# A gated delta rule in eleven pipelined stages: gates as 32 more value columns, two-part logs, 19-column weights, and another order at each stage's start

## The chip, the cores and the metric

The kernel runs on one core of one Trainium2 chip. The metric is device microseconds from start to end of one execution. Engines: PE (TensorE, matmuls; PEld is its weight load), DVE (VectorE), ACT (ScalarE), POOL (GpSimd) and SP, which issues DMAs. Each has its own queue and runs it in order; they meet by semaphores. PE's granted clock stands at one of two levels, 1.2 and 2.4 GHz, shown as 0.5 and 1.0.

## The reference

A two-layer tower over 64 images with 38 tokens of 256 features. Only the attention of the second layer changes. It is a recurrence over the 38 tokens of an image, per head (16 heads of 16 features):

```
q, k, v = silu(x @ Wq), l2norm(silu(x @ Wk)), silu(x @ Wv)
gk      = log_sigmoid(x @ Wf)               # one number per token and head
a       = k * -sigmoid(x @ Wgamma) * exp(gk)
for t in tokens:
    Sp = S * exp(gk[t])
    u  = a[t] @ Sp + v[t]
    S  = Sp + outer(k[t], u)
    o[t] = q[t] @ S
```

After it come a gate (sigmoid of a rank-16 product), a layer norm, the product with Wo and the second feed-forward.

## The kernel before

**The method.** No loop runs over tokens. With decays D[t, s] = exp(sum of gk between s and t), u solves (I - A) u = v, where A[t, s] = D (a_t . k_s), and o = (D (q . k)) u. The inverse of I - A is built row by row for the two halves of 19 tokens; the halves are joined by a remainder.

**The stages.** Images are worked off in 8 chunks of 8 (`CB`); a chunk is four pairs of images (`IP`), so 64 lanes of image pair and head. `last_layer` first normalises and transposes x (`layer_norm_turn`, which also loads and splits the weights into a high and a low fp32r part), then calls `delta_stage` eleven times (`CHUNKS + 3`). One stage works on four chunks at once, each a step further on:

- `nxt` (stages 0 to 7): `project` makes q, k and the two gates with features on partitions, in 8 projections of 6 matmuls of 304 columns; `sigmoid`, `silu_of`, then the norm of the keys (`square` on POOL, `key_norm` on PE, `bounded`, `inverse_norms`, `unit_key`), `gates` and `a_of` for a.
- `c` (stages 1 to 8): `values` makes v and the forget logit (24 matmuls of 272 columns); `forget_parts`, `forget_logs`, `log_forget` give gk; `steps` on POOL, `decay` on PE and ACT give D; `score` on PE and `weigh` on DVE give q.k and a.k times D in `PA`.
- `z` (stages 2 to 9): `a_rows` on PE turns A so that lanes stand on partitions (banks 0 and 1), a copy by ACT and one by DVE bring it into `AS`; `inverse_row(1..18)` on DVE, each a product and a reduction, each waiting for the one before; `inverse_out` and `inverse_back` turn the inverse back into `TS`.
- `y` (stages 3 to 10): `first_half`, `first_back`, `remainder`, `with_values`, `second_half`, `solution` solve for u (banks 0 and 1); `output` gives o, and `high_out` and `low_out` write it as two parts.

Stages 3 to 7 hold all four and are called full; a middle stage is one of 4 to 7. A stage ends with a barrier of all engines, and the first product of the next needs the last `weigh`.

**The order.** It is written out by hand: the last lines of the four engine programs call those functions one after another (before: lines 1625 to 1664 for PE, 1781 to 1819 ACT, 1950 to 1990 DVE, 2041 to 2063 POOL). Scores use banks 0 to 3 alone, so `score(p + 1)` waits for `weigh(2p)` and `weigh(2p + 1)`, and they for it. `steps(b + 2)` waits for `decay(b)` of PE, `decay(b + 2)` for it.

## Time and profile before

| | |
|---|---|
| runs | median 2027.8 us (2023.66, 2027.8, 2028.45) |
| the profiled execution | 2023.3 us, span 2021.3 |
| busy, whole span | PE 1769.4, DVE 1084.5, ACT 672.3, POOL 299.6 us |
| normalisation ahead of the stages | 1280.9 to 1304 us |
| stages 0 to 10 | 1304 to 1850 us |
| PE's first matmul in stages 3 to 8 | 1399.8, 1466.8, 1529.7, 1593.0, 1656.7, 1720.5 |
| mean granted clock | 0.876 of 2.4 GHz |

Times in a timeline count from the span's start. A wait is named by what ended it; "issue" is time in which the engine waited for nothing that the profile shows. A group's busy time adds durations, which overlap a little on one engine, so the distance from start to start is the better price of an instruction in a row of them.

### The profile page before, as it was taken

The numbers are of one execution on the slowest core, as the hardware profiler recorded it, in microseconds if no ns is written. First come the engines' busy times: TensorE is split into PE (matmuls) and PEld (weight loads), VectorE is DVE, ScalarE is ACT, GpSimd is POOL, SyncE is SP. The second block draws the span as 40 slices with busy tenths as digits, with TensorE's granted clock in tenths as the row PEclk, the third lists the DMA queues.
The fourth block names the chain that finished last, engine by engine and source line by source line (L and its number), as shares of the span: only waits on it lengthen the run. The fifth ranks groups of instructions, "written<-read, shape, count | busy, mean of one in ns | idle before, by whom it ended". The sixth has DMA issues, their size and how long they took to land. (4 is left out here: it accounts for less than half of the span.)

```text
span 2021.3 us, 52149 instructions
## 1 busy us (share of the span) xinstructions
PE 1769.4 (88%) x22817; PEld 1573.1 (78%) x22817; DVE 1084.5 (54%) x2346; ACT 672.3 (33%) x1389; POOL 299.6 (15%) x302
## 2 busy tenths in 40 slices
PE   5677786799999999999999999778999889777589
PEld 4466675579888999999999989566788778767468
DVE  3655555584546545545555455545534454442885
ACT  3344444432223222223223232354333333223133
POOL 0322232610000000000000000332222222100540
PEclk9788898899999999999999999788776877655579
DMA  4100000100001000000000000100000000001001
GB/s 142 50 2 1 0 0 2 65 21 22 22 1 43 1 22 21 22 22 22 22 21 22 1 1 1 34 2 2 3 4 3 3 3 4 4 4 47 1 7 44
DMA packets 9943, 36.03 MB, mean 18 GB/s; under 512 B 3056, under 2 KB 5896, under 8 KB 7176
## 3 DMA queue, kind: packets, MB, share of 16 engines
q1 hardware_dynamic: 9736, 32.96, 4.7%
q8 instruction: 167, 2.74, 0.6%
q14 instruction: 40, 0.33, 0.1%
HBM read 30.47 MB, written 2.49 MB: 16 GB/s over the span
## 5 line engine op out<-in xcount | busy, mean ns | idle before, releaser
L1042 ACT ACTIVATE hidden<-bank,moe_b 128x512 f32<-128x512 f32 (+1 forms) x320 | 213.3, 668 | 537.1 <-PE bank L934 526.1
L951 PE MATMUL bank<-moe_w2h,hidden_hi 128*128 128x256 f32 x1216 | 345.7, 284 | 0.0
L951 PE MATMUL bank<-moe_w2l,hidden_hi 128*128 128x256 f32 x1216 | 344.0, 283 | 0.0
L951 PE MATMUL bank<-moe_w2h,hidden_lo 128*128 128x256 f32 x1216 | 344.0, 283 | 0.0
L934 PE MATMUL bank<-x_hi,moe_w1h 128*128 128x512 f32 (+1 forms) x640 | 243.8, 381 | 2.9 <-ACT hidden L1042 2.8
L934 PE MATMUL bank<-x_lo,moe_w1h 128*128 128x512 f32 (+1 forms) x640 | 242.5, 379 | 0.0
L934 PE MATMUL bank<-x_hi,moe_w1l 128*128 128x512 f32 (+1 forms) x640 | 242.0, 378 | 0.0
L951 PEld LDWEIGHTS bank<-moe_w2h,hidden_hi 128*128 128x128 f32 x1216 | 233.1, 192 | 5.9 <-DVE residual L1076 4.3
L951 PEld LDWEIGHTS bank<-moe_w2l,hidden_hi 128*128 128x128 f32 x1216 | 233.2, 192 | 1.2
L951 PEld LDWEIGHTS bank<-moe_w2h,hidden_lo 128*128 128x128 f32 x1216 | 233.2, 192 | 0.0
L1076 DVE SCALAR_TENSOR_TENSOR residual<-bank,gates,residual 128x256 f32<-128x256 f32 x152 | 73.4, 484 | 290.4 <-PE bank L951 290.4
L1064 DVE TENSOR_TENSOR hidden_lo<-hidden,hidden_hi 128x512 fp32r<-128x512 f32 (+1 forms) x320 | 215.2, 672 | 11.0
L1062 DVE CAST hidden_hi<-hidden 128x512 fp32r<-128x512 f32 (+1 forms) x320 | 133.1, 416 | 87.3 <-ACT hidden L1042 79.9
L934 PEld LDWEIGHTS bank<-x_hi,moe_w1h 128*128 128x128 f32 x640 | 120.3, 188 | 25.8 <-ACT hidden L1042 5.0
L934 PEld LDWEIGHTS bank<-x_hi,moe_w1l 128*128 128x128 f32 x640 | 120.1, 188 | 20.4
L934 PEld LDWEIGHTS bank<-x_lo,moe_w1h 128*128 128x128 f32 x640 | 120.3, 188 | 18.7
L1249 POOL MEMSET gate_low<- 80x2432 f32 x1 | 2.1, 2121 | 867.1 <-POOLq L68 867.1
L167 PE MATMUL bank<-ident,normed_tiles 128*128 128x128 f32 x152 | 49.7, 446 | 47.6 <-DVE normed_tiles L136 47.6
L167 PEld LDWEIGHTS bank<-ident,normed_tiles 128*128 128x128 f32 x152 | 22.5, 204 | 74.1 <-DVE normed_tiles L136 74.0
L2008 POOL TENSOR_TENSOR decay_steps<-normed_tiles,from_here 128x304 f32<-128x304 f32 x64 | 50.5, 804 | 139.6 <-PE bank L1506 73.9
L1902 DVE TENSOR_TENSOR qk_and_ak<-bank,decay 128x304 f32<-128x304 f32 x128 | 52.2, 466 | 22.5 <-ACT decay L1722 17.0
L831 POOL TENSOR_TENSOR probs<-probs,row_inv 128x608 f32<-128x608 f32 x32 | 38.7, 1209 | 167.1 <-DVE row_inv L715 166.9
(284 smaller groups left out, 3531.5 us busy)
## 6 DMA issues: line engine op xcount, KB each, us to landing
moe_w<-in_moe_w SPq DMA_DIRECT2D x16, 1024.0 KB, 4.8
patches<-in_patches SPq DMA_DIRECT2D x8, 864.0 KB, 4.5
out<-residual SPq DMA_DIRECT2D x19, 128.0 KB, 1.7
ffn_w<-in_ffn_w SPq DMA_DIRECT2D x2, 1024.0 KB, 6.4
att_w<-in_att_w SPq DMA_DIRECT2D x1, 1536.0 KB, 5.9
delta_w<-in_delta_w SPq DMA_DIRECT2D x1, 1280.0 KB
tok_w<-in_tok_w SPq DMA_DIRECT2D x1, 768.0 KB, 4.1
delta_wvf<-in_delta_wvf SPq DMA_DIRECT2D x1, 272.0 KB
```

Source lines behind the costliest of these rows:

```text
L167: turn = nc.tensor.transpose(bank[t % 4][:, m * P:(m + 1) * P], XN[:, t % 4, m * P:(m + 1) * P], ident[:, :])
L831: nc.gpsimd.tensor_tensor(PR[:, p % 2, :, 0:SEQ], PR[:, p % 2, :, 0:SEQ], spread(RI[:, p % 2, :], 2, SEQ), ALU.mult).then_inc(normed, 1)
L934: mm = nc.tensor.matmul(bank[i % 4][:, 0:n], left, right, start=(j == 0), stop=(j == len(passes) - 1))
L951: mm = nc.tensor.matmul(bank[4 + n % 3][:, 0:D], left, right, start=(i == 0), stop=(i == len(passes) - 1))
L1042: nc.scalar.activation(H[:, i % 4, 0:n], bank[i % 4][:, 0:n], ACT.Relu, bias=b1[:, x, f:f + 1]).then_inc(acted, 1)
L1062: nc.vector.tensor_copy(HH[:, k % 2, f, 0:n], H[:, i % 4, 0:n]).then_inc(h_hi, 1)
L1064: nc.vector.tensor_tensor(HL[:, k % 2, f, 0:n], H[:, i % 4, 0:n], HH[:, k % 2, f, 0:n].bitcast(F32), ALU.subtract).then_inc(h_lo, 1)
L1076: nc.vector.scalar_tensor_tensor(out=RES[:, t, :], in0=bank[4 + n % 3][:, 0:D], scalar=G[:, t, x:x + 1], in1=RES[:, t, :], op0=ALU.mult, o ...
L1249: nc.gpsimd.memset(G1[:].bitcast(F32), 0.0).then_inc(done, 1)
L1902: nc.vector.tensor_tensor(PA[:, c % 2, p, m * HPH:(m + 1) * HPH].rearrange("p (g e) x t -> p e g x t", e=2)[:, e], psum[:, 0:PPH, n * 2 * ...
L2008: nc.gpsimd.tensor_tensor(MS[:, b % 2], spread(LZ[:, 3, b // 2, b % 2 * HPH:(b % 2 + 1) * HPH], 2, SEQ), spread(here[:, :], 1, HPH), ALU.m ...
```

## The change

- **Gates.** The two gate projections per half (4 of 8 projections) go, and so do `gates` and `a_of`. The weight of `values` gets 16 more columns (Wgamma, one per head), so v, forget logit and gamma logit come as token rows: 288 columns. `step_scale` makes g = -sigmoid(gamma) sigmoid(f) for 64 lanes. PA then holds k.k in place of a.k, and g is applied where rows are turned: `a_rows` turns g too (4 matmuls more), and `a_out` on DVE copies it and multiplies the 18 rows by it in one product of 684 elements, in place of the two copies; `with_values` becomes two products on DVE.
- **Split logs.** gk is split into two fp32r parts, `steps` writes both (608 elements for 304), and `decay` adds two fp32r matmuls in place of one fp32 matmul. Four decay buffers stand for two; v has three for two.
- **19-column weights.** `first_half` and `second_half` load 19 columns of `TS` for 32.
- **The order.** See below. In the normalisation, two weight splits fewer follow, which move two tiles later with the wait for the loads.

```diff
-        wh = sb(ctx, "delta_wh", [P, 5, HALVES, D], F32R)
+        wh = sb(ctx, "delta_wh", [P, 3, HALVES, D], F32R)
-DECAYS = 2
+DECAYS = 4
+KINDS = D + 2 * HEADS
...
-        "MS": sb(ctx, "decay_steps", [P, 2, HPH, SEQ]),
+        "MS": sb(ctx, "decay_steps", [P, 2, 2, HPH, SEQ], F32R),
...
-    jobs = ((K, 0), (K, 1), (Q, 0), (Q, 1), (GAMMA, 0), (F, 0), (GAMMA, 1), (F, 1))
+    jobs = ((K, 0), (K, 1), (Q, 0), (Q, 1))
...
-                nc.tensor.matmul(bank[4 + b % 2][:, 0:CT], after[:, :],
-                                 MS[:, b % 2].rearrange("p g t -> p (g t)"),
-                                 start=False, stop=True).then_inc(d_log, 1)
+                for part in range(2):
+                    mm = nc.tensor.matmul(bank[4 + b % 2][:, 0:CT], after[:, :],
+                                          MS[:, b % 2, part].rearrange("p g t -> p (g t)"),
+                                          start=False, stop=(part == 1))
+                mm.then_inc(d_log, 1)
...
+                for r in range(4):
+                    nc.tensor.matmul(psum[half(r // 2), r % 2, 0:HALF],
+                                     GZ[block_rows(r), z % 3].rearrange("p i g -> p (i g)"),
+                                     ident[block_rows(r), r * HB:r * HB + HALF], start=True, stop=True)
...
             def first_half(j):
...
                 if z is not None:
-                    pe.wait_ge(a_taken, 2)
+                    pe.wait_ge(a_taken, 1)
...
-                        mm = nc.tensor.matmul(psum[rows, j, place(lane)],
-                                              TS[rows, lane * HALF:lane * HALF + HB], vh_y[rows, lane, :],
+                        mm = nc.tensor.matmul(psum[PAD * s:PAD * s + HALF, j, place(lane)],
+                                              TS[rows, lane * HALF:(lane + 1) * HALF], vh_y[rows, lane, :],
...
-            def a_of_second():
+            def a_out():
...
-                nc.vector.tensor_copy(AS[:, 1, 1:HALF].rearrange("p t s -> p (t s)"),
-                                      bank[1][:, HALF:HALF * HALF]).then_inc(a_taken, 1)
+                nc.vector.tensor_copy(AS[:, :, 0, :], psum[:, 0:2, 0:HALF]).then_inc(scale_in, 1)
+                dve.wait_ge(scale_in, 1)
+                nc.vector.tensor_tensor(AS[:, :, 1:HALF, :],
+                                        psum[:, 0:2, HALF:HALF * HALF].rearrange("p h (t s) -> p h t s", s=HALF),
+                                        spread(AS[:, :, 0, 1:HALF], 3, HALF), ALU.mult).then_inc(a_taken, 1)
...
+            def step_scale():
...
+                nc.vector.scalar_tensor_tensor(
+                    out=GZ[:, c % 3], in0=SV[:, :, D + HEADS:KINDS], scalar=-1.0, in1=SV[:, :, D:D + HEADS],
+                    op0=ALU.mult, op1=ALU.mult).then_inc(scale_ready, 1)
...
-                nc.vector.tensor_tensor(RX[:, lanes(j), :], vh_y[:, lanes(j), :],
-                                        bank[j][:, :].rearrange("p (l d) -> p l d", d=HD),
+                scale = GZ[:, y % 3].rearrange("p i g -> p (i g)")
+                nc.vector.tensor_tensor(RX[:, lanes(j), :], bank[j][:, :].rearrange("p (l d) -> p l d", d=HD),
+                                        spread(scale[:, lanes(j)], 2, HD), ALU.mult).then_inc(r_scaled, 1)
+                dve.wait_ge(r_scaled, j + 1)
+                nc.vector.tensor_tensor(RX[:, lanes(j), :], RX[:, lanes(j), :], vh_y[:, lanes(j), :],
                                         ALU.add).then_inc(rx_ready, 1)
...
-                nc.gpsimd.tensor_tensor(MS[:, b % 2], spread(LZ[:, 3, b // 2, b % 2 * HPH:(b % 2 + 1) * HPH], 2, SEQ),
-                                        spread(here[:, :], 1, HPH), ALU.mult).then_inc(steps_ready, 1)
+                heads = slice(b % 2 * HPH, (b % 2 + 1) * HPH)
+                nc.gpsimd.tensor_tensor(MS[:, b % 2], spread(LF[:, :, b // 2, heads].bitcast(F32), 3, SEQ),
+                                        spread(spread(here[:, :], 1, HPH), 1, 2), ALU.mult).then_inc(steps_ready, 1)
```

**PE, how a full stage comes to its first solution product.** Before, the stage opens with `a_rows` (L1549), and the values' 24 matmuls (L1492) stand between it and the first half (L1581); a projection (L1474) follows.

```order
L1492 MATMUL bank<-delta_wvfl,dchunk_hi 128x272
L1492 MATMUL bank<-delta_wvfh,dchunk_lo 128x272
L1581 MATMUL bank<-values,inverse_t 32x16 x128
L1474 MATMUL bank<-x_hi,delta_wh 128x304
L1474 MATMUL bank<-x_lo,delta_wh 128x304
```

The same place now. Values and projections 0 and 1 (L1476) open the stage.

```order
L1476 MATMUL bank<-x_lo,delta_wh 128x304
L1476 MATMUL bank<-x_hi,delta_wl 128x304
L1551 MATMUL bank<-ident,step_scale 64x19 x4
L1557 MATMUL bank<-ident,qk_and_ak 64x19 x72
L1589 MATMUL bank<-values,inverse_t 19x16 x128
L1601 MATMUL bank<-u_then_rest,qk_and_ak 19x16 x64
```

The turn of the coefficients has moved right before the first half, which has 19 columns, and the remainder (L1601) follows at once.

**PE, around the output product.** Before, the output (L1621) and four projections are followed by key norms (L1483), two decays (L1504, L1506), a score (L1528) and a turn of the inverse (L1564).

```order
L1474 MATMUL bank<-x_hi,delta_wl 128x304
L1483 MATMUL bank<-k_square_then_norm,same_head 128x304 x2
L1504 MATMUL bank<-past,ident_bf_8 128x304
L1506 MATMUL bank<-decay_steps,after 128x304
L1504 MATMUL bank<-past,ident_bf_8 128x304
L1506 MATMUL bank<-decay_steps,after 128x304
L1528 MATMUL bank<-q_and_a_92,dk_in_pair 64x76 x32
L1564 MATMUL bank<-ident,inverse 64x64 x16
```

Now (L1613 is the second half, L1629 the output, L1485 the key norms, L1506 and L1509 a decay, L1532 a score):

```order
L1613 MATMUL bank<-u_then_rest,inverse_t 19x16 x64
L1506 MATMUL bank<-past,ident_bf_8 128x304
L1509 MATMUL bank<-decay_steps,after 128x304 x2
L1613 MATMUL bank<-u_then_rest,inverse_t 19x16 x64
L1506 MATMUL bank<-past,ident_bf_8 128x304
L1509 MATMUL bank<-decay_steps,after 128x304 x2
L1485 MATMUL bank<-k_square_then_norm,same_head 128x304 x2
L1629 MATMUL bank<-qk_and_ak 32x38 x128
L1506 MATMUL bank<-past,ident_bf_8 128x304
L1509 MATMUL bank<-decay_steps,after 128x304 x2
L1532 MATMUL bank<-q_and_k_91,dk_in_pair 64x76 x32
```

Two decays and the key norms stand ahead of the output, and no projection stands behind it.

**DVE, behind the output's low parts.** Before (L1922 the low parts, L1837 and L1840 a row of the inverse, L1874 the bounded norms, L1902 a weighing product):

```order
L1922 TENSOR_TENSOR x_lo<-bank,x_hi 128x4x38 x4
L1837 TENSOR_TENSOR normed_tiles<-a_rows,inverse 128x2x14x14
L1840 TENSOR_REDUCE inverse<-normed_tiles 128x2x14
L1874 TENSOR_SCALAR k_square_then_norm<-bank 128x304 x2
L1837 TENSOR_TENSOR normed_tiles<-a_rows,inverse 128x2x15x15
L1840 TENSOR_REDUCE inverse<-normed_tiles 128x2x15
L1902 TENSOR_TENSOR qk_and_ak<-bank,decay 128x4x76 x2
L1837 TENSOR_TENSOR normed_tiles<-a_rows,inverse 128x2x16x16
```

Now (L1918 the low parts, L1832 and L1835 a row, L1895 a weighing product, L1882 the unit keys):

```order
L1918 TENSOR_TENSOR x_lo<-bank,x_hi 128x4x38 x4
L1832 TENSOR_TENSOR normed_tiles<-a_rows,inverse 128x2x13x13
L1835 TENSOR_REDUCE inverse<-normed_tiles 128x2x13
L1832 TENSOR_TENSOR normed_tiles<-a_rows,inverse 128x2x14x14
L1835 TENSOR_REDUCE inverse<-normed_tiles 128x2x14
L1895 TENSOR_TENSOR qk_and_ak<-bank,decay 128x4x76 x4
L1832 TENSOR_TENSOR normed_tiles<-a_rows,inverse 128x2x15x15
L1835 TENSOR_REDUCE inverse<-normed_tiles 128x2x15
L1882 TENSOR_TENSOR q_and_k_91<-q_and_k_91,k_square_then_norm 128x8x38 x2
L1832 TENSOR_TENSOR normed_tiles<-a_rows,inverse 128x2x16x16
```

The bounded norms have left this place, row 13 has come in, and behind row 16 stand two weighing pairs and rows 17 and 18, then the last four pairs in a row; before, the a-products stood between them.

## Rows read from the trace of the kernel before

**Rows 1.** Windows, one stage each: us, then PE, PEld, DVE, ACT, POOL busy, PEclk
```profile
1354.00:1398.00 44.00, 35.15 (x576) 29.49 (x576) 27.31 (x69) 18.76 (x45) 11.57 (x16) 0.84 0.01 2
1398.00:1465.00 67.00, 60.12 (x1600) 53.64 (x1600) 28.97 (x75) 22.35 (x55) 14.26 (x18) 0.69 0.01 3
...
1591.50:1655.00 63.50, 56.53 (x1600) 50.26 (x1600) 28.75 (x75) 22.23 (x55) 14.27 (x18) 0.76 0.01 3
```

**Rows 2.** Windows of PE alone, the middle stage: us, PE busy, PEclk
```profile
1610.00:1632.00 22.00, 22.00 (x681) 0.50 0.02 4
...
1636.00:1655.00 19.00, 16.61 (x369) 1.00 0.01 3
```

**Rows 3.** Timeline of PE, middle stage: start, us, line, x count [idle before <-releaser]
```profile
1593.04 5.06 PE L1549 MATMUL bank<-ident,qk_and_ak 32*64 32x19 f32 x144 [2.62 <-PEq L68]
...
1602.98 3.17 PE L1581 MATMUL bank<-values,inverse_t 32*32 32x16 f32 x189
...
1616.47 0.62 PE L1474 MATMUL bank<-x_hi,delta_wh 128*128 128x304 f32 x1
...
1618.29 3.60 PE L1605 MATMUL bank<-u_then_rest,inverse_t 32*32 32x16 f32 x128
...
1634.27 1.10 PE L1621 MATMUL bank<-qk_and_ak 64*32 64x38 f32 x103 [1.85 <-issue]
```

**Rows 4.** Timeline of PE, the stage without projections
```profile
1737.51 2.31 PE L1593 MATMUL bank<-u_then_rest,qk_and_ak 32*19 32x16 f32 x128 [1.62 <-issue]
1740.98 1.48 PE L1593 MATMUL bank<-u_then_rest,qk_and_ak 32*19 32x16 f32 x79 [1.16 <-issue]
...
1744.45 3.60 PE L1605 MATMUL bank<-u_then_rest,inverse_t 32*32 32x16 f32 x128 [0.82 <-issue]
```

**Rows 5.** Timeline of DVE, the middle stage
```profile
1598.16 0.52 DVE L1827 COPY a_rows<-bank 128x342 f32<-128x342 f32 x1 [6.03 <-PE bank L1549]
...
1627.25 0.51 DVE L1837 TENSOR_TENSOR normed_tiles<-a_rows,inverse 128x338 f32<-128x338 f32 x1
...
1643.71 1.21 DVE L1837 TENSOR_TENSOR normed_tiles<-a_rows,inverse 128x578 f32<-128x578 f32 x1
...
1654.14 1.62 DVE L1902 TENSOR_TENSOR qk_and_ak<-bank,decay 128x304 f32<-128x304 f32 x4 [1.10 <-ACT decay L1722]
```

**Rows 6.** Groups of DVE, tail of the middle stage: busy us, mean ns | idle before, releaser
```profile
L1902 DVE TENSOR_TENSOR qk_and_ak<-bank,decay 128x304 f32<-128x304 f32 x16 | 6.5, 466 | 2.7 <-ACT decay L1722 2.7
L1837 DVE TENSOR_TENSOR normed_tiles<-a_rows,inverse 128x392 f32<-128x392 f32 (+4 forms) x5 | 3.9, 779 | 0.0
L1840 DVE TENSOR_REDUCE inverse<-normed_tiles 128x28 f32<-128x392 f32 (+4 forms) x5 | 3.5, 692 | 0.2
...
L1874 DVE TENSOR_SCALAR k_square_then_norm<-bank 128x304 f32<-128x304 f32 x2 | 0.9, 470 | 0.3 <-PE bank L1483 0.3
...
L1888 DVE SCALAR_TENSOR_TENSOR q_and_a<-dk_t,sig_gamma 128x304 f32<-128x304 f32 x2 | 0.8, 466 | 0.0
```

**Rows 7.** Timeline of POOL there, and from the page a 608-element product
```profile
1643.61 0.70 POOL L2008 TENSOR_TENSOR decay_steps<-normed_tiles,from_here 128x304 f32<-128x304 f32 x1 [2.75 <-PE bank L1506]
...
L831 POOL TENSOR_TENSOR probs<-probs,row_inv 128x608 f32<-128x608 f32 x32 | 38.7, 1209 | 167.1 <-DVE row_inv L715 166.9
```

**Rows 8.** Timeline of PE, first stage with values and no inverse
```profile
1325.86 0.57 PE L1492 MATMUL bank<-delta_wvfh,dchunk_hi 128*128 128x272 f32 x1 [4.03 <-PEq L68]
...
1334.74 0.41 PE L1474 MATMUL bank<-x_hi,delta_wh 128*128 128x304 f32 x1 [2.61 <-DVE dk_t L1856]
```

**Rows 9.** Timeline of DVE, the very first stage
```profile
1321.03 0.47 DVE L1874 TENSOR_SCALAR k_square_then_norm<-bank 128x304 f32<-128x304 f32 x1 [1.21 <-PE bank L1483]
```

**Rows 10.** Timeline of DVE, the normalisation ahead of the stages
```profile
1289.51 0.61 DVE L1237 TENSOR_SCALAR delta_w<-delta_w,norm_w 128x256 f32<-128x256 f32 x2 [1.86 <-DMA from_here<-in_from_here]
...
1293.52 0.40 DVE L136 TENSOR_SCALAR normed_tiles<-residual,mean_var,std 128x256 f32<-128x256 f32 x1
...
1296.81 1.03 DVE L136 TENSOR_SCALAR normed_tiles<-residual,mean_var,std 128x256 f32<-128x256 f32 x1
```

More of the change, by code:

```diff
@@ L1221, in last_layer @@
         same = sb(ctx, "same_head", [P, P])
-        after = sb(ctx, "after", [P, P])
+        after = sb(ctx, "after", [P, P], F32R)
         past = sb(ctx, "past", [P, SEQ], BF16)
@@ L1258, in last_layer @@
                             splits=[(wg[:], wgh[:], wgl[:]), (wvf[:], wvfh[:], wvfl[:])]
-                            + [(w[:, n], wh[:, n], wl[:, n]) for n in range(5)])
+                            + [(w[:, n], wh[:, i], wl[:, i]) for i, n in enumerate((0, 1, 4))])
         with ExitStack() as inner:
@@ L1380, in delta_buffers @@
         "PA": sb(ctx, "qk_and_ak", [P, 2, IP, HEADS, 2, SEQ]),
-        "VH": sb(ctx, "values", [P, 2, IP, HEADS, HD]),
-        "QA": [sb(ctx, f"q_and_a{i}", [P, HALVES, CB, 2, SEQ]) for i in range(2)],
-        "KT": sb(ctx, "dk_t", [P, HALVES, CB, SEQ]),
+        "VH": sb(ctx, "values", [P, 3, IP, HEADS, HD]),
+        "QK": [sb(ctx, f"q_and_k{i}", [P, HALVES, CB, 2, SEQ]) for i in range(2)],
         "SH": sb(ctx, "dchunk_hi", [P, HALVES, CB, PAD], F32R),
@@ L1628, in _ @@
             low_part(0)
+            low_part(1)
+            project(0)
+            project(1)
+            a_rows()
             first_half(0)
             first_half(1)
-            project(0)
-            low_part(1)
+            low_part(2)
             remainder(0)
-            project(1)
-            low_part(2)
-            remainder(1)
             project(2)
             low_part(3)
-            second_half(0)
+            remainder(1)
             project(3)
             low_part(4)
+            second_half(0)
+            decay(0)
             second_half(1)
-            project(4)
-            project(5)
-            output()
-            project(6)
-            project(7)
+            decay(1)
             key_norm(0)
             key_norm(1)
-            decay(0)
-            decay(1)
+            output()
+            decay(2)
             score(0)
+            decay(3)
             inverse_out(0)
-            decay(2)
+            decay(4)
+            score(1)
+            decay(5)
             inverse_out(1)
-            decay(3)
-            score(1)
+            decay(6)
+            score(2)
+            decay(7)
             inverse_out(2)
-            decay(4)
-            decay(5)
-            score(2)
-            decay(6)
-            decay(7)
             score(3)
@@ L1950, in _ @@
             decay_masks()
-            a_of_second()
+            log_forget()
+            silu_of(0)
+            silu_of(1)
+            a_out()
             for t in range(1, 6):
                 inverse_row(t)
-            log_forget()
-            inverse_row(6)
-            with_values(0)
-            silu_of(0)
-            inverse_row(7)
-            with_values(1)
-            silu_of(1)
             values_of(0)
             values_of(1)
-            inverse_row(8)
-            silu_of(2)
             values_of(2)
             values_of(3)
-            inverse_row(9)
+            with_values(0)
+            silu_of(2)
+            with_values(1)
             silu_of(3)
             gate_parts()
-            for t in range(10, 14):
+            step_scale()
+            for t in range(6, 10):
+                inverse_row(t)
+            bounded(0)
+            bounded(1)
+            for t in range(10, 13):
                 inverse_row(t)
```

186 lines of the change are left out of this document (80 added, 106 removed).

## Prediction

> **What bounds the kernel now.** The change lies in the eleven delta stages and in the normalisation just ahead of them; nothing behind them is touched. I read the windows by stage first, then one middle stage engine by engine, then the ends. The windows [rows 1] show the first full stage at 67.0 us and a later one at 63.5, PE busy for 60.1 and 56.5 of it, DVE for 29. PE is the engine to follow, but its granted clock is now at one of its levels, now at the other: 0.50 (1.2 GHz) over 22 us of small matmuls, 1.00 (2.4 GHz) over the last 19 us [rows 2]. The timeline of PE [rows 3] splits a middle stage in two. **Front**, from the first matmul (1593.04) to the end of the output product (1634.27 + 1.10 = 1635.37): 42.3 us. **Tail**, from there to DVE's last product (1654.14 + 1.62 = 1655.76 [rows 5]): 20.4 us. In the front PE is hardly idle; in the tail it is DVE that hardly rests: of 20 us it waits 3.2 [rows 6].
>
> Two more things hide in the front. A small matmul costs by the columns of its weights: 128 with 32 columns take 3.60 us, 128 with 19 take 2.31 [rows 3, 4], 10 ns less each. And PE runs dry: the output product is broken by an "issue" idle of 1.85 us [rows 3]. In the stage without projections [rows 4] the pieces between such idles hold 128 records and start at 1737.51, 1740.98 and 1744.45: twice 3.47 us apart, however fast the piece was (2.31 us and 1.16 idle; then 2.65 and 0.82). I read this as the supply of PE's instructions: **no block of 128 records starts sooner than 3.47 us after the last.** (An fp32 product counts double in these records: 72 in the code are x144 [rows 3].)
>
> **A middle stage, front.** Values come first now, then projections 0 and 1. The stage that has this order already took from 1325.86 to 1332.13 for them (1334.74 less the idle of 2.61 [rows 8]): 6.3, less 0.2 of modelled overhang, plus 0.25 for 16 more columns in 24 matmuls: 6.35. The turns of the coefficients: 5.06 us for 144 [rows 3], now 152: 5.3. Then a new wait: the first solution product writes the two banks that DVE has to empty, and where the values stood between (1598.10 to 1602.98, 4.9 us [rows 3]) nothing does now. DVE makes a copy of 38 elements and a product of 684; a copy of 342 took 0.52 [rows 5], so 0.2 + 0.9 and hand-overs: 1.3, bounds 1.0 (the product alone) and 1.8 (at 1.5 times its price). Behind it on PE is the whole rest of the front.
>
> From there to the output's end PE has four times 256 small records, projections 2 and 3 (12), two decays (6) and the key norms (4): 1046 records, 8.17 blocks, 28.4 us at 3.47. By duration alone it would be less: 768 records of 19 columns are 6 x 2.31 = 13.9, the output 2.7 (1.10 for 103 [rows 3]), projections 3.6 (1616.47 to 1618.29 [rows 3], twice), norms and decays about 4.5: 25. So **the narrower weights gain next to nothing; the blocks take it back.** Three blocks with dense matmuls exceed 3.47 (by 0.4, 0.4 and 1.2), the cut ones at both ends are quicker (1.2): 29.2, bounds 25 and 32. Front: 6.35 + 5.3 + 1.3 + 29.2 = 42.15, against 42.3. The four projections that go (7.3 us by those rows) pay for the wait and for the norms and decays that now stand ahead of the output; the rest of them ran beside refills.
>
> **Tail.** DVE's list changes so [rows 6]: the bounded norms leave (0.9 + 0.3 of wait), the a-products leave (0.8), of the 2.7 us of waits before weighing products the last of 1.10 [rows 5] stays, 1.6 go, because two decays are done early, four decay buffers stand for two, and rows 17 and 18 stand beside a score. Row 13 comes in, 2 x 0.51 [rows 5]. POOL's steps hold 608 elements for 304: 0.70 becomes 1.2 (the page's 608-element product), bounds 1.2 and 1.6 [rows 7]. They are off the path, six of them in 18 us, but DVE's product of two SBUF operands that met one (both near 1643.7) took 1.21 us, and the five products of such rows 3.9 against 3.5 for their five reductions [rows 5 to 7]: 0.4 a meeting, which at the new length is 0.7. Four of the six steps can meet one: 2.8 at most, 0.4 is in already; I add 0.8, a third of the rest. Sum: 20.4 - 1.2 - 0.8 - 1.6 + 1.05 + 0.8 = 18.65, bounds 17.8 and 20.3. PE keeps up: of its 16.6 us in the last 19 [rows 2] the norms, two projections and two decays leave. The decays' fp32 products become two fp32r ones: nothing on the path. Between the stages nothing changes. **A middle stage gains 0.15 + 1.8, so 2.0 us, times four: 8.** The first full stage, 67.0 long [rows 1] where the others are near 63.5, lands with them at 61.5: 5.5.
>
> **The other stages.** The one with the first inverse (44.0 [rows 1]) is DVE's: coefficients ready at 6.35 + 5.3 + 1.3 = 12.95, then its 27.3 us less the evacuation, the a-products and what now runs earlier (0.5 + 0.8 + 1.1), 1.4 of hand-overs, a score 1.1, 1.0 between stages: 40.3, gain 3.7. The first with values: 24 projections of 304 columns at 2.4 GHz 3.0, a-products 0.8, and 1.2 of the 2.61 wait [rows 8], as the sigmoids of the keys no longer stand behind those of the values: 5.0. The very first: DVE was free 1.21 us before the key norms [rows 9], and the a-products go: 2.0. The last three: the blocks hold, the wait comes in, one more row in the tail, two decays fewer in one: 0.8 lost. The normalisation: DVE waited 1.86 us for loads, which now it does two tiles of 0.65 later: 1.3; its products took 1.03 instead of 0.40 while POOL split weights [rows 10], two splits fewer: 1.25; one copy more, 0.15: 2.4. **Sum: 2.4 + 2.0 + 5.0 + 3.7 + 5.5 + 8 - 0.8 = 25.8.** The profiled execution took 2023.3 us, near the fastest run; the median is 2027.8. I take the gain off the median: **2002.**
>
> **Rivals.** (1) *The full stages give nothing*: the wait is 1.8 and POOL meets every product. For it: [rows 5 to 7]. Then 25.8 - 8 - 3 = 15 remain, 2013; inside my range. (2) *No block rule*: blocks are buffered well ahead, the front falls by 4.2 us to its matmuls in five stages and by 7 in two of the last: 35 more, 1967. Against it stand the idles themselves [rows 3, 4]. The Trainium skill, Runtime: NRT & Kernel Launch, Instruction fetch mechanics, says that instructions come in blocks of 256 and that crossing a boundary is "mostly hidden"; by that rule the time is this rival's. The trace disagrees with "hidden" (1.16 us of a block), though 128 matmuls with their loads do make 256. (3) *Slower*: POOL's steps and DVE's products take turns in full. Eight steps of 1.6 instead of 0.7 add 7 us to DVE in each of eight stages, 57 - 26: 2059. It decides from 3.2 us a stage on. Against it: the weighing products, over a third of DVE's tail, read PSUM, and 0.4 of a 0.70 step was felt. The Trainium skill, SBUF — State Buffer, Who interferes with whom, lets a product of two SBUF inputs wait for a whole POOL instruction; by it a meeting costs 1.2, some 2 us more a stage, 2018. (4) *No difference*: the tail at 1.2 GHz. The dense projections that stood before it are gone; PE's 11 us of tail become up to 21, past DVE's 18.6, 3 us a stage in eight stages: 2026.
>
> **Chances.** Forecast 0.68, rival 1 0.16, rival 2 0.05, rival 3 0.04, rival 4 0.07. The range 1986 to 2018 holds the first two and with them 0.84; the bounds of the front (25 and 32, in five stages) would reach farther, at the lower end to rival 2. A measurement here tells 0.3%, 6 us, from no change: faster 0.90, same 0.05, slower 0.05.
>
> **What would show it.** Middle stages of 61 to 62 us, front 42, tail 18 to 19; PE idle for 1.3 us ahead of the first 19-column product; "issue" idles in nearly every block of the front, 3.47 us from start to start; one late wait of DVE instead of three; steps of 1.2 to 1.6 on POOL. I am wrong if blocks follow faster than 3.47, or if the tail doesn't shorten.

## The result, and the profile after

The changed kernel takes 2012.81 us, the median of four runs (2009.08 to 2015.91), and the kernel before 2027.22, the median of four as well (2023.66 to 2028.45; one run more than in the table ahead of the change): a ratio of 0.9931, 95% interval 0.9907 to 0.9955. That is 14.4 us less, where 25.8 were forecast. The time lies in the range, the sign is right, and the gain is little more than half of what the working gave. 2013 was the time of the first rival, "the full stages give nothing", and the trace says the same, though only one half of that rival's reasons holds.

The profiled execution took 2014.98 us, with a span of 2013.2. Stage by stage, from PE's first matmul to that of the next stage (for the normalisation, from DVE's first operation to its last), the two traces give:

| | before | after | gained | forecast |
|---|---|---|---|---|
| normalisation | 23.1 | 21.0 | 2.1 | 2.4 |
| stage 0 | 21.2 | 19.5 | 1.7 | 2.0 |
| stage 1 | 30.0 | 25.7 | 4.3 | 5.0 |
| stage 2, first inverse | 44.0 | 44.5 | -0.5 | 3.7 |
| stage 3, first full | 67.0 | 61.4 | 5.5 | 5.5 |
| stages 4 to 7, mean | 63.4 | 63.9 | -0.5 each | 2.0 each |
| stages 8 to 10 together | 132.2 | 132.9 | -0.7 | -0.8 |

The sum is 10.5 us. Both traces show one thing more that no edit explains: in the unchanged code ahead of the normalisation the profiled execution of after is 2.4 us later. So the two profiled spans differ by 8.1 us (2021.3 and 2013.2) and the medians by 14.4: the table places the gain of one execution of each, and some 6 us of the medians' difference stand in no row of it.

Of before, timeline of DVE: the first operation of the normalisation.

```profile
1280.94 2.11 DVE L119 TENSOR_SCALAR std<-mean_var 128x19 f32<-128x19 f32 x1 [0.78 <-PEq L68]
```

Of after, timeline of DVE, the same operation, the scaled weights and a product of a tile beside a split by GpSimd, which answer to [rows 10].

```profile
1283.34 2.11 DVE L119 TENSOR_SCALAR std<-mean_var 128x19 f32<-128x19 f32 x1 [0.78 <-PEq L68]
...
1292.25 0.61 DVE L1237 TENSOR_SCALAR delta_w<-delta_w,norm_w 128x256 f32<-128x256 f32 x2 [0.90 <-DMA from_here<-in_from_here]
...
1301.00 1.02 DVE L136 TENSOR_SCALAR normed_tiles<-residual,mean_var,std 128x256 f32<-128x256 f32 x1
```

The wait for the loads is 0.90 us for 1.86, and four products took 1.0 us for six.

**The middle stage.** Windows of after by stage (us; PE, PEld, DVE, ACT, POOL busy; PEclk), the answer to [rows 1]: PE is busy for 50.4 us of 62.9, where it was busy for 56.5 of 63.5. Six microseconds of work on the fullest engine are gone, and the stage is as long as it was.

```profile
1350.10:1394.60 44.50, 31.22 (x560) 27.74 (x561) 29.95 (x70) 17.00 (x41) 13.58 (x15) 0.73 0.01 2
1394.60:1456.00 61.40, 50.04 (x1584) 44.59 (x1585) 32.11 (x78) 20.42 (x51) 16.40 (x17) 0.67 0.02 4
1584.80:1647.70 62.90, 50.35 (x1584) 45.10 (x1584) 33.12 (x78) 20.68 (x50) 16.31 (x16) 0.66 0.01 3
```

Timeline of PE in that stage, the answer to [rows 3].

```profile
1584.81 0.58 PE L1494 MATMUL bank<-delta_wvfh,dchunk_hi 128*128 128x288 f32 x1 [2.68 <-PEq L68]
...
1592.53 5.04 PE L1557 MATMUL bank<-ident,qk_and_ak 32*64 32x19 f32 x144
...
1598.79 2.74 PE L1589 MATMUL bank<-values,inverse_t 32*19 32x16 f32 x153 [1.22 <-DVE a_rows L1821]
...
1602.43 1.81 PE L1589 MATMUL bank<-values,inverse_t 32*19 32x16 f32 x98 [0.90 <-issue]
...
1605.90 1.91 PE L1601 MATMUL bank<-u_then_rest,qk_and_ak 32*19 32x16 f32 x103 [1.23 <-issue]
...
1613.63 2.32 PE L1613 MATMUL bank<-u_then_rest,inverse_t 32*19 32x16 f32 x128
...
1616.75 2.32 PE L1613 MATMUL bank<-u_then_rest,inverse_t 32*19 32x16 f32 x128
...
1621.60 1.32 PE L1629 MATMUL bank<-qk_and_ak 64*32 64x38 f32 x129
1624.04 1.30 PE L1629 MATMUL bank<-qk_and_ak 64*32 64x38 f32 x127 [1.12 <-issue]
...
1643.70 1.40 PE L1532 MATMUL bank<-q_and_k,dk_in_pair 32*64 32x76 f32 x64 [0.56 <-DVE qk_and_ak L1895]
```

The reader sees the new wait, 1.22 us, as forecast; "issue" idles between the small products, with 3.47 us from 1602.43 to 1605.90; two second halves, each of 128 records, that start only 3.12 us apart (1613.63, 1616.75), and 129 output records that are followed by the next after 2.44 us (1621.60, 1624.04), both sooner than the 3.47 of the prediction's rule; and, at the end, a score that took 1.40 us, where one at 2.4 GHz takes 0.95. Values and projections 0 and 1 took 7.58 us (1584.81 to 1592.39; 7.2 in the mean of stages 4 to 7), for 6.35 in the sum.

Windows of PE alone in after (us, PE busy, PEclk): [rows 2] had 1.00 in the tail; here the whole tail has 0.72 and its last 7 us have 0.50.

```profile
1625.34:1646.82 21.48, 14.30 (x351) 0.72 0.01 3
...
1639.82:1646.82 7.00, 3.81 (x111) 0.50 0.01 2
```

Timeline of DVE in that tail, the answer to [rows 5].

```profile
1630.09 1.61 DVE L1895 TENSOR_TENSOR qk_and_ak<-bank,decay 128x304 f32<-128x304 f32 x4 [1.04 <-PE bank L1532]
1631.62 1.01 DVE L1832 TENSOR_TENSOR normed_tiles<-a_rows,inverse 128x450 f32<-128x450 f32 x1
...
1633.20 1.86 DVE L1882 TENSOR_TENSOR q_and_k<-q_and_k,k_square_then_norm 128x304 f32<-128x304 f32 x2
1634.99 1.70 DVE L1832 TENSOR_TENSOR normed_tiles<-a_rows,inverse 128x512 f32<-128x512 f32 x1
...
1638.85 0.75 DVE L1832 TENSOR_TENSOR normed_tiles<-a_rows,inverse 128x578 f32<-128x578 f32 x1
...
1645.20 1.62 DVE L1895 TENSOR_TENSOR qk_and_ak<-bank,decay 128x304 f32<-128x304 f32 x4 [1.55 <-issue]
```

The larger product of row 17 (578 elements) took 0.75 us, that of row 16 (512) 1.70. Timeline of POOL, beside it:

```profile
1630.94 1.21 POOL L2003 TENSOR_TENSOR decay_steps<-log_f_parts,from_here 128x608 fp32r<-128x608 f32 x1 [0.99 <-PE bank L1509]
1633.46 2.68 POOL L2003 TENSOR_TENSOR decay_steps<-log_f_parts,from_here 128x608 fp32r<-128x608 f32 x2 [1.31 <-PE bank L1509]
```

Two steps stand from 1633.46 to 1636.14, over the unit keys and the product of row 16, and the step before them, to 1632.15, over the beginning of row 15 (450 elements); no other product of this tail is late. What a product lost is nearly what was left of the step when it started: 0.4 of 0.53 us for row 15, 1.0 of 1.15 for row 16. A product that takes longer because a step runs beside it is called a meeting here, as in the prediction. Two suspects, then, for the tail: GpSimd's longer steps, and PE's clock. The question of the experiments is which, and whether they are one.

### The profile page after: what moved, and what is told of

It reads as the page before. It is cut to its first block and busy times, and to the rows that moved or that the text cites. A ratio compares the mean times of both kernels' runs of the same rounds, so it can differ in the third digit from the quotient of the medians.

```text
span 2013.2 us, 51796 instructions
## 1 busy us (share of the span) xinstructions
PE 1715.6 (85%) x22689; PEld 1525.8 (76%) x22689; DVE 1110.8 (55%) x2379; ACT 657.8 (33%) x1347; POOL 314.5 (16%) x284
## 5 line engine op out<-in xcount | busy, mean ns | idle before, releaser
L934 PEld LDWEIGHTS bank<-x_hi,moe_w1h 128*128 128x128 f32 x640 | 120.3, 188 | 25.8 <-ACT hidden L1042 5.0
L2003 POOL TENSOR_TENSOR decay_steps<-log_f_parts,from_here 128x608 fp32r<-128x608 f32 x64 | 78.5, 1236 | 150.1 <-PE bank L1509 113.0
L1832 DVE TENSOR_TENSOR normed_tiles<-a_rows,inverse 128x2 f32<-128x2 f32 (+5 forms) x144 | 67.6, 469 | 3.5
```

What stands on the lines that cost most here:

```text
L934: mm = nc.tensor.matmul(bank[i % 4][:, 0:n], left, right, start=(j == 0), stop=(j == len(passes) - 1))
L1832: nc.vector.tensor_tensor(PD[:, :, 0:t, 0:t], spread(AS[:, :, t, 0:t], 2, t), TT[:, :, 0:t, 0:t], ALU.mult).then_inc(t_mult, 1)
L2003: nc.gpsimd.tensor_tensor(MS[:, b % 2], spread(LF[:, :, b // 2, heads].bitcast(F32), 3, SEQ), spread(spread(here[:, :], 1, HPH), 1, 2), AL ...
```

## The experiments

Each kernel is the changed one with the edit shown. Times are set against the kernel before, run on the same chip, since its median moved between 2027.2 and 2025.1; a difference to the changed kernel is that of the ratios, times 2025. Its uncertainty is some 5 to 6 us, most of it from the changed kernel's own interval.

**The narrow weights undone.**

```diff
-mm = nc.tensor.matmul(psum[PAD * s:PAD * s + HALF, j, place(lane)],
-                      TS[rows, lane * HALF:(lane + 1) * HALF], vh_y[rows, lane, :],
+mm = nc.tensor.matmul(psum[PAD * s:PAD * s + HB, j, place(lane)],
+                      TS[rows, lane * HALF:lane * HALF + HB], vh_y[rows, lane, :],
```

(and so in `second_half`).

> The changed kernel with one part undone: the two halves of the solution load 32 columns of the inverse again, for 19. My theory (blocks of 128 records start no sooner than 3.47 us after one another): 128 such matmuls cost 3.60 us for 2.32, but the blocks of 19 columns end 1.1 us before the next may start, so that only 3.60 - 3.47 = 0.13 us of each is seen, four blocks a stage, seven stages: about +4 us, 2013 to 2018. The idle called issue in the front (3.9, 6.7, 4.7, 3.3 and 5.2 us in the five full stages) shrinks by some 4 us a stage. Rival (a matmul's price is what the front pays): 512 x 10 ns = 5.1 us a stage, seven stages and some: +36 to +41 us, about 2050.

Measured: 2023.46 us, 0.9984 (0.9975 to 0.9993), 10.7 us more than the changed kernel. In stages 4 to 7 the path from the first solution product to the output's end grew by 1.6 us in the mean (29.0 to 30.7), and the "issue" idle of a stage fell from 5.5 to 2.2. Timeline of PE:

```profile
1602.02 6.85 PE L1589 MATMUL bank<-values,inverse_t 32*32 32x16 f32 x250 [1.22 <-DVE a_rows L1821]
...
1617.14 3.60 PE L1613 MATMUL bank<-u_then_rest,inverse_t 32*32 32x16 f32 x128
...
1621.54 3.60 PE L1613 MATMUL bank<-u_then_rest,inverse_t 32*32 32x16 f32 x128
```

Of 5.1 us that 512 matmuls save by their own duration, a stage sees 1.6: the rest was waiting for instructions anyway. My theory had 0.5, the rival 5. The theory was too even: from one second half to the next PE took 4.40 us here (1617.14 to 1621.54) and 3.12 in the changed kernel, all that the narrow ones save, where six and three dense matmuls stand ahead of them and neither has an "issue" idle before it. From the first solution product to the projection behind the first remainder it saved 0.3 us (9.2 here, 8.95 in the changed kernel): the "issue" idles took the rest. The time itself lies between the two expectations, 5 us above the first and 27 below the second.

**Each remainder product issued twice.**

```diff
+for _ in range(2):
     mm = nc.tensor.matmul(psum[PAD * s + HB:PAD * s + HB + HALF, j, place(lane)],
                           pa_y[rows, lane, 1, HALF:SEQ], RX[rows, lane, :],
                           start=True, stop=True)
```

> The changed kernel with each of the 128 products of a remainder issued twice (the same result written twice): 256 small records of 19 columns more in each of eight stages. Block theory (no block of 128 records starts sooner than 3.47 us after the last): 2 x 3.47 = 6.9 us a stage, +55 us, about 2068, although DVE, ACT and GpSimd do nothing more. Price theory (a record costs its 17.5 to 18 ns): 256 x 18 ns = 4.6 us a stage, +37, about 2050; and if the idle called issue takes some of them in, less.

Measured: 2074.21 us, 1.0238 (1.022 to 1.0256): 62 us more than the changed kernel, in eight stages 7.8 each in the mean, for 256 records. Stages 4 to 7 grew by 6.9 us, which is twice 3.47; stages 3 and 8 grew by 10.3 and 9.5, for which the rule of the blocks has no reason. Timeline of PE:

```profile
1626.11 1.81 PE L1589 MATMUL bank<-values,inverse_t 32*19 32x16 f32 x98 [0.72 <-issue]
...
1629.58 2.32 PE L1602 MATMUL bank<-u_then_rest,qk_and_ak 32*19 32x16 f32 x128 [1.23 <-issue]
1633.05 1.92 PE L1602 MATMUL bank<-u_then_rest,qk_and_ak 32*19 32x16 f32 x103 [1.15 <-issue]
```

1626.11, 1629.58 and 1633.05 stand 3.47 us apart, twice, and a row of 128 narrow products takes 2.32 of it. So in a long row of them the price of a small matmul is the pace at which they come, 27 ns, and not its 18 ns on PE. That the pace is that of the instruction supply is my reading: "issue" says only that the profile shows nothing that PE waited for. The Trainium skill, Runtime: NRT & Kernel Launch, Instruction fetch mechanics, calls the crossing of a block of 256 instructions "mostly hidden"; in such a row 1.15 to 1.23 us of each block of 128 matmuls are not, and the measurement decides. Behind dense matmuls my rule doesn't hold: the second halves of the changed kernel came 3.12 us apart.

**The split logs undone.** Steps are one fp32 tile again, and a decay adds one fp32 product.

```diff
-for part in range(2):
-    mm = nc.tensor.matmul(bank[4 + b % 2][:, 0:CT], after[:, :],
-                          MS[:, b % 2, part].rearrange("p g t -> p (g t)"),
-                          start=False, stop=(part == 1))
+mm = nc.tensor.matmul(bank[4 + b % 2][:, 0:CT], after[:, :],
+                      MS[:, b % 2].rearrange("p g t -> p (g t)"),
+                      start=False, stop=True)
...
-nc.gpsimd.tensor_tensor(MS[:, b % 2], spread(LF[:, :, b // 2, heads].bitcast(F32), 3, SEQ),
-                        spread(spread(here[:, :], 1, HPH), 1, 2), ALU.mult)
+nc.gpsimd.tensor_tensor(MS[:, b % 2], spread(LZ[:, 3, b // 2, heads], 2, SEQ),
+                        spread(here[:, :], 1, HPH), ALU.mult)
```

> The changed kernel with one part undone: the steps are one fp32 tile of 304 elements for two fp32r ones of 608, and a decay adds one fp32 product. GpSimd's steps take 0.70 us for 1.21. Theory A (the steps and DVE's products of two SBUF operands take turns): the stage with the first inverse, where five of DVE's operations beside four steps in a row took 0.6 to 1.0 us more each than alone, comes down from 44.5 to about 42.5; in full stages the products of 450 and 512 elements and the unit keys lose about half of the 2.0 us that they have too much: 1 us a stage; total -6 to -8, 2005 to 2007. Theory B (the tail is held by PE at 1.2 GHz and by score and weighing in turn): full stages the same, only the second stage moves: 2010 to 2013.

Measured: 1996.08 us, 0.9856 (0.984 to 0.9871), 15 us less than the changed kernel, twice what theory A had. The second stage came to 40.5 us, where the prediction had 40.3. The tails of stages 4 to 7 came from 20.3 to 17.8. Timeline of DVE, the same operations as above:

```profile
1614.31 1.62 DVE L1890 TENSOR_TENSOR qk_and_ak<-bank,decay 128x304 f32<-128x304 f32 x4 [0.19 <-PE bank L1531]
...
1617.04 0.85 DVE L1877 TENSOR_TENSOR q_and_k<-q_and_k,k_square_then_norm 128x304 f32<-128x304 f32 x2
1617.81 0.69 DVE L1831 TENSOR_TENSOR normed_tiles<-a_rows,inverse 128x512 f32<-128x512 f32 x1
```

0.85 for 1.86 and 0.69 for 1.70. And a window of PE over the last 7 us of that tail:

```profile
1621.51:1628.51 7.00, 4.10 (x146) 1.00 0.01 4
```

The clock is back at 2.4 GHz, though nothing dense was added. So either of the two suspects could have done it, and a next run has to part them.

**Short work, long steps.** As the last, but a step writes its product twice.

```diff
-nc.gpsimd.tensor_tensor(MS[:, b % 2], spread(LZ[:, 3, b // 2, heads], 2, SEQ), spread(here[:, :], 1, HPH), ALU.mult)
+nc.gpsimd.tensor_tensor(MS[:, b % 2], spread(spread(LZ[:, 3, b // 2, heads], 2, SEQ), 1, 2),
+                        spread(spread(here[:, :], 1, HPH), 1, 2), ALU.mult)
```

> The kernel with the split logs undone, with one thing added: GpSimd's steps write their product twice (608 elements, of which the decay's fp32 product reads 304), so that they take 1.2 us again while PE's and DVE's work stays that of the undone split. Theory A (the length of GpSimd's steps beside DVE is what the split logs cost): back to 2008 to 2014, the second stage to 44.5. Theory C (the two fp32r products, or the two more operations of DVE on the logs, are what they cost): stays at 1995 to 1999.

Measured: 2011.82 us, 0.994 (0.9924 to 0.9956): the time of the changed kernel. Tails 19.7, second stage 43.8. Timelines of DVE and of POOL:

```profile
1635.05 1.70 DVE L1831 TENSOR_TENSOR normed_tiles<-a_rows,inverse 128x512 f32<-128x512 f32 x1
```

```profile
1634.78 1.42 POOL L1998 TENSOR_TENSOR decay_steps<-normed_tiles,from_here 128x608 f32<-128x608 f32 x1 [1.55 <-PE bank L1508]
```

This run decides most: what the split logs cost, 15 us, is the length of GpSimd's steps. The matmuls and the two more operations on the logs cost nothing that the intervals show, which is to say less than some 6 us in all.

**PE kept busy in the tail.** The long steps stay; six more mask products stand ahead of each of decays 4 to 7, into a bank that the decay then overwrites.

```diff
+for _ in range(6 if b in (4, 5, 6, 7) else 0):
+    nc.tensor.matmul(bank[4 + b % 2][:, 0:CT], identb[:, :], spread(past[:, :], 1, HPH), start=True, stop=True)
```

> The changed kernel with six more dense products (the mask product of 128x304, its result overwritten) ahead of each of decays 4 to 7, 24 a stage, where PE waits for DVE anyway; the output is the same. Theory B (clock): the last 7 us of the full stages' tails, granted 0.50 in four of five, come to 1.00; scores 2 and 3 take 0.95 for 1.40 us each, decays 0.7 for 1.2, the wait of DVE before the last weighing (1.55) shrinks by 0.45: tail 20.3 to about 19, and the next stage's values and projections, which began at 1.2 GHz (7.2 us for 6.35), gain up to 0.8: -1.5 to -2 us a stage, 2002 to 2006. Theory A (DVE's tail is full of its own and of GpSimd's work): the clock rises and the time stays, 2011 to 2014, or is longer by the filler (24 x 0.13 = 3 us a stage at most, 2030) if PE was the bound.

Measured: 2002.9 us, 0.9888 (0.9873 to 0.9903): with 24 more matmuls a stage it is 8.7 us less. Window of PE over the last 7 us of stage 6's tail, then two rows of DVE's timeline:

```profile
1628.63:1635.63 7.00, 5.28 (x160) 1.00 0.01 2
```

```profile
1627.26 1.35 DVE L1835 TENSOR_TENSOR normed_tiles<-a_rows,inverse 128x578 f32<-128x578 f32 x1
...
1634.01 1.62 DVE L1898 TENSOR_TENSOR qk_and_ak<-bank,decay 128x304 f32<-128x304 f32 x4 [1.35 <-issue]
```

The clock is up, and DVE still meets a step (1.35 us for 0.75). Tails came from 20.3 to 19.3 and fronts from 42.7 to 41.0. That 1 us of the tail is not the price of the clock, though, for the filler moved the steps as well: the last two wait for decays 4 and 5, which now come behind filler. What DVE's operations in a middle tail took over the shortest time of the same operation is 2.1 us in the mean in the changed kernel, 0.1 with short steps, 1.9 with the long ones of the run before, and 1.15 here. So the meetings fell by 1.0, all that the tail gained, while the waits before weighing products fell from 1.8 to 1.7. With short steps they are 1.2, and the 2.6 us that short steps gave in the tail are 2.0 of meetings and 0.6 of waits. Runs and traces fit this order of cause: a long step delays DVE, DVE delays the weighing for which PE waits, PE idles more (7.2 us of stage 6's tail, 4.8 with short steps: 21.48 less 14.30, 18.10 less 13.30), and its clock falls; only then is the last score slow. That the length of the step starts it is shown by the run before; the links behind it are not tested one by one, and the filler's run does not part the clock from the meetings.

**The turn of the coefficients first.**

```diff
+a_rows()
 for p in range(IP):
     values(p)
...
 project(0)
 project(1)
-a_rows()
```

(and DVE's `a_out` and rows 1 to 5 ahead of `log_forget`).

> The changed kernel with one part undone: a stage begins with the turn of the coefficients again (and DVE with their copy and the first five rows of the inverse), values and two projections follow. If the new wait of 1.23 us ahead of the first solution product is what the new order costs, it is hidden in stages 3 to 9, 8 to 9 us in all, and the second stage, which is DVE's, gets its coefficients 7 us earlier and loses its empty start: 44.5 to 41 or 42. Total about 2001 to 2004. Rival: values, logs and steps come 5 us later, and the decays and the output's neighbours wait for them: the gain of the front is given back in the tail, 2011 to 2015.

Measured: 1997.49 us, 0.9858 (0.9843 to 0.9873), 15 us less than the changed kernel, and more than either theory had. In stages 4 to 7 the time to the first solution product is 11.6 us for 13.6, and from there to the output's end 27.8 for 29.0. That is 3.3 a stage, where the wait was 1.2. The second stage came to 43.0 us for 44.5.

**The turn between values and projections.**

```diff
 for p in range(IP):
     values(p)
+a_rows()
...
 project(0)
 project(1)
-a_rows()
```

> The changed kernel with its values first, but with the turn of the coefficients ahead of projections 0 and 1 and not behind them, so that 12 dense products stand between the turn and the first solution product. If the wait of 1.23 us and the cold start of the first half are what the order of the change costs, this gives the same as the turn at the very start did, 1997 to 2001 (stages 3 to 7: from start to the first solution product 11.9 for 13.6). If the earlier start of the inverse was what helped there, less: 2003 to 2010.

Measured: 2011.86 us, 0.9929 (0.9912 to 0.9946): nothing gained, where one theory had 1997 to 2001 and the other 2003 to 2010. The wait is hidden there as well, and yet the first solution product comes 14.0 us after the start. The pair tells what the wait alone could not. Windows of PE (us, busy, PEclk), first with the turn first, from the stage's start: the turn, the next 2.8 us of values, the rest of values and projections, the first solution products.

```profile
1575.94:1581.20 5.26, 5.26 (x153) 0.50 0.01 3
1581.20:1584.00 2.80, 2.80 (x12) 0.50 0.00 0
1584.00:1587.50 3.50, 3.50 (x26) 0.98 0.00 0
1587.50:1591.00 3.50, 2.10 (x154) 0.99 0.02 5
```

Then with the turn between (values; turn; projections):

```profile
1583.00:1590.00 7.00, 5.28 (x22) 0.50 0.00 0
1590.00:1595.00 5.00, 5.00 (x144) 0.84 0.01 3
1595.00:1600.00 5.00, 5.00 (x96) 0.50 0.00 0
```

And in the changed kernel (beginning of values; the rest and the projections; turn; first solution products):

```profile
1584.80:1588.00 3.20, 3.19 (x13) 0.50 0.00 0
1588.00:1592.40 4.40, 4.40 (x27) 0.71 0.00 0
1592.40:1597.60 5.20, 5.17 (x153) 0.98 0.02 3
1598.80:1602.00 3.20, 2.73 (x153) 0.50 0.03 5
```

In each of the three PE starts the stage at 1.2 GHz and comes to 2.4 in or behind its dense matmuls. The turn cannot use it: its 144 records took 5.04 us at 0.98 and 5.04 at 0.50. In the changed kernel the 2.4 GHz falls in large part on the turn; with the turn between, the projections behind it are at 1.2 GHz again; only with the turn first do the clocked-up microseconds fall on the rest of the dense ones and on the first solution products. From start to start, in the mean of stages 4 to 7, values and projections take 7.2 us in the changed kernel, 6.4 with the turn first and 8.9 with the turn between, and the turn 5.1 to 5.2 in all three. That and the wait make up the three starts of 13.6, 11.6 and 14.0. Tails are alike (20.1 with the turn first, 20.0 with it between), so the earlier start of the inverse gives nothing to a full stage; in the second stage it gives 1.8 us (43.0, and 44.8 with the turn between).

The faster first solution products give nothing that can be seen: in stage 6, 153 records took 2.09 us instead of 2.74, and the "issue" idle behind them 1.91 instead of 0.90. Nor does the order explain why the way from the first solution product to the output's end is 27.8 us for 29.0. It is 27.8 with the turn between as well, where nothing was gained in all, and in the filler's run; from stage to stage it goes from 26.6 to 31.2 in the changed kernel. Its cause stays open.

**Both undone, and what else might be had.** Short steps and the turn first:

> Two parts of the change undone together: the split logs, and the order at a stage's start (turn of the coefficients first). Alone they gave 16.7 and 15.3 us against the changed kernel. The one was in the tails (20.3 to 17.8 us a full stage) and the second stage, the other in the fronts (42.4 to 39.6), so they should add: 1979 to 1984, full stages near 58. If they share a cause (a tail that ends at 2.4 GHz and so a faster start), only part adds: 1986 to 1992.

Measured: 1989.56 us, 0.9829 (0.9813 to 0.9845): 21 us less than the changed kernel, not 30 (the 16.7 and 15.3 of the expectation are differences of medians, 15 and 15 by ratios). Alone the two gave a middle stage 3.4 and 3.5 us, together 4.2; the second stage 4.0 and 1.5, together 2.8. Tails are 18.1; but the start took 12.3 us for the 11.6 of the turn first alone, as more of the values ran at 1.2 GHz. That the two share the clock, in part, is how I read it; no run shows it by itself. Three mask products more ahead of each of decays 4 to 7:

> Both parts undone, and three dense products more ahead of each of decays 4 to 7, 12 a stage. With short steps the tails' last 7 us were already granted 0.87 to 1.00, so if the clock was lost only because PE waited for a delayed DVE, the filler has nothing to give: within 3 us of the same kernel without it, or longer by its 12 x 0.13 us a stage (8 us). If some clock is still lost (values first no longer warm the front), -3 to -6.

Measured: 1985.74 us, 0.9818 (0.98 to 0.9835): 2 us less, within the intervals. Where the steps are short PE keeps its clock nearly by itself (0.84 to 1.00 in the last 7 us without the filler). Six buffers of steps for two, all filled right behind the logs:

```diff
-for b in range(2):
+for b in range(6):
     steps(b)
```

> Both parts undone, and GpSimd's steps have six buffers for two: six of eight are made right behind the logs, and only two fall into the tail. If what is left of the contention still costs (0.3 to 0.4 us where a 450-element product met a 0.70 us step), the full stages lose another 0.3 to 0.6 us and the second stage 0.5: -2 to -4 against the same kernel with two buffers. If the six in a row hold DVE's first rows or the copy of the coefficients instead, it is the same or slower by 1 to 3.

Measured: 1986.95 us, 0.9821 (0.9802 to 0.9839), again 2 us less and within the intervals, although tails are the shortest of all, 17.6. All together:

> All that helped together: fp32 steps of 304 elements in six buffers, the turn of the coefficients first, three dense products more ahead of each of decays 4 to 7. Alone, the last two gave 2.6 and 3.8 us on the version without them (1989.6). If they add: 1982 to 1985. If they share the cause, a late PE in the tail: 1985 to 1988.

Measured: 1987.33 us, 0.9811 (0.9796 to 0.9825). The four kernels with both parts undone cannot be told apart, at 35 to 38 us below the kernel before. With the turn between instead:

> As the run before, with the turn of the coefficients between values and projections. The logs and steps start 5 us earlier, the inverse 2 us later. DVE's tail is what sets a full stage's end and both are ready by then: within 3 us of the run before. In the second stage, which is DVE's, the coefficients come later: +1 to +2 there.

Measured: 1999.47 us, 0.9867 (0.9849 to 0.9885), 11 us more than the run before it, where 3 were expected at most. The middle stages are 61.6 us for 59.6, nearly all of it in the start (13.5 for 12.2) and behind it. The place of the turn is worth 11 us in this company and 14 in the other.

What wasn't tried: narrow weights alone in the kernel before; the gates as value columns alone; long steps in more buffers; and a rest of the tail in which DVE waits before its last weighing products in every version (1.1 to 1.6 us).

## Why the prediction was right and wrong

**Held.** The ends: normalisation, stages 0, 1, 3 and 8 to 10 gained 12.9 us together, where the sum had 14.1. The new wait was 1.22 for 1.3. From the first solution product to the output's end the middle stages took 29.0 us in the mean, 5.0 of them "issue" idles, and the sum had 29.2, by blocks; by durations alone it had 25. So rival 2, with its 1967, fell, and "the narrower weights gain next to nothing" held in direction: 1.6 of 5.1 us a stage, 10.7 in all.

**The signs.** The prediction named two signs of being wrong: "if blocks follow faster than 3.47, or if the tail doesn't shorten". Both came. Second halves of 128 records followed after 3.12 us, and idles did not stand in nearly every block: the 3.47 us hold in a row of small matmuls alone. The mean of 29.0 came out even so, from stages of 26.6 to 31.2, and its closeness to 29.2 is partly luck. And the tail went from 20.3 us to 20.3, where 18.65 was forecast. This is what took the gain of the middle stages away.

**Failed: DVE and POOL in the tail.** The step was "I add 0.8, a third of the rest". It took the price of one meeting at the old length (0.4) in proportion to the new one (0.7), and a third of the chances. The meetings of the profiled stage 6 cost 2.4 us: 0.4 on the 450, 1.0 on the 512 elements and 1.0 on the unit keys, over their durations without a step beside them (0.62, 0.69, 0.85). The sum held 0.4 and 0.8. Over the four middle stages it is 2.1 in the mean (1.2 to 2.6), for 1.2. Without its 0.8 the working gives 17.85 us for the tail, and the run with short steps had 17.8. A meeting is not worth a share of a step's length: the DVE product waited for nearly all that was left of the step, 1.0 us of 1.15. The Trainium skill, SBUF — State Buffer, Who interferes with whom, lets a DVE product of two SBUF inputs wait for the whole GpSimd instruction; the trace agrees. The 2 us a stage more that I had worked out from it and left aside make 3.2 of meetings, and 2018: nearer to the 2.4 of stage 6 and to the time than the 1.2 and the 2002 of my sum, and too much in its turn.

A second term of the tail failed with it: "of the 2.7 us of waits before weighing products ... 1.6 go". In stage 6 they were 1.04 and 1.55, so 2.6, nearly what they had been; in the other three middle stages one wait of 1.55 was left for the 1.10 of the sum. The last score of stage 6 took 1.40 us for 0.95.

**Failed: the second stage.** The 40.3 us were right for short steps (40.5 measured), with luck: the terms as they are written add up to 41.35 (12.95 + 27.3 - 2.4 + 1.4 + 1.1 + 1.0). They were 4.2 too few for long steps, since there four steps follow one another beside DVE. Timeline of POOL in after, and of DVE:

```profile
1367.61 4.73 POOL L2003 TENSOR_TENSOR decay_steps<-log_f_parts,from_here 128x608 fp32r<-128x608 f32 x4 [6.51 <-PE bank L1509]
```

```profile
1367.83 1.08 DVE L1852 SCALAR_TENSOR_TENSOR step_scale<-sig_v 128x64 f32<-128x64 f32 x1
1368.82 1.26 DVE L1832 TENSOR_TENSOR normed_tiles<-a_rows,inverse 128x72 f32<-128x72 f32 x1
...
1370.38 0.89 DVE L1832 TENSOR_TENSOR normed_tiles<-a_rows,inverse 128x98 f32<-128x98 f32 x1
...
1371.60 0.89 DVE L1832 TENSOR_TENSOR normed_tiles<-a_rows,inverse 128x128 f32<-128x128 f32 x1
```

Alone these take 0.21, 0.23, 0.26 and 0.29 us: 3.1 us lost to one row of steps. The sum had no term for contention in this stage at all, though the same operations stood in it.

**Failed: the clock.** Rival 4 had the mechanism, PE losing the dense projections ahead of the tail, and a price of 3 us a stage, with 0.07. It came half true: the last 7 us of four middle tails were granted 0.67, 0.50, 0.50 and 0.50 where they had 1.00. Its reason was too simple, since nearly the same PE work with short steps kept 0.87 to 1.00. And the sum priced values and projections at 6.35 us from a stage in which they came to 2.4 GHz sooner; here they took 7.2, and much of the 2.4 GHz was spent on the turn.

**The account.** The profiled difference of 10.5 us lacks 15.3 of 25.8: 9.9 in the middle stages, 4.2 in the second, 1.2 in the rest. In a middle stage the forecast was 42.15 and 18.65 (a gain of 1.9 that was rounded to 2.0), the mean is 42.65 and 20.34: 0.85 too little for the start and 1.7 for the tail. The traces give the 1.7 almost whole: 0.9 of meetings (2.1 for 1.2), 0.45 of the last wait (1.55 for 1.10), 0.25 of stage 6's wait of 1.04, spread over four. The forecast itself, 2002, missed by 10.8 us. It would have missed by more on the profiled pair alone: the median of after is lower than its profiled run (2012.8, 2015.0), that of before higher. The range held since it was made to reach to rival 1, and the time came out as that rival's.

So with both parts undone the rest of the change brings 35 us; the split logs and the order, 15 us each alone, take 21 of them away together, and 14 are left. That the narrow weights help is shown; that the gates as value columns do rests on the sum of stages 0, 1 and 3 and on no run of its own.

## What to carry to other kernels

Before an operation of GpSimd is made longer, look for the DVE products of two SBUF operands beside it and count for each the whole rest of the step that it can meet; to test it, lengthen the step without using the result. Ask of dense matmuls not only what they cost but where the clock that they raise is spent, and put work that cannot use it (here the turn, 5.04 us at either level) ahead of them, not behind. Where the gaps between small matmuls come at even distances, count records, not durations, and count them only in long rows of small matmuls. And before a filler's gain is put down to the clock, see whether it also moved other engines.

## What the runs showed of the hardware

A filler can pay: 24 matmuls of 128x304 a stage, whose results are thrown away, took 8.7 us off the whole. DVE and GpSimd delay each other both ways: beside DVE's products a step of 304 elements took 1.23 us for its usual 0.70, one of 608 took 1.42 for 1.21. The records of the turn (64 rows, 19 columns) cost 35 ns at either level of the clock. The 3.47 us between the starts of 128 small matmuls and the next came back to the hundredth in three kernels, in long rows of them; behind dense ones the next came sooner, after 3.12 us (128 records) and 2.44 us (129).
